# A mixture-of-experts router in three phases instead of two, with TensorE's table words loaded between the first blocks

## What is computed

```python
x = x + _L0_xattn_ref(_layernorm(x), ctx, ctx, mask, wo_w, wo_b)   # relu(softmax(q k + mask) v @ wo.T + b)
xf = _layernorm(x).reshape(-1, 256)
scores = softmax(xf @ gw + gb)                                     # (896, 32)
group_scores = sum(top_k(scores.reshape(T, 8, 4), 2))              # keep the 4 best groups
weights, indices = top 4 of the kept scores
for e in experts:  y += w_e * ((silu(xf @ w1e + b1e) * (xf @ w3e + b3e)) @ w2e + b2e)
z = (silu(xf @ sw1 + sb1) * (xf @ sw3 + sb3)) @ sw2 + sb2          # the shared expert
x = x + y + z
```

## Time and profile before

| | us |
|---|---|
| median of 3 runs | 327.31 (327.04 to 328.64) |
| the profiled execution, its own time | 327.03 |
| its span, first to last instruction | 325.3 |
| PE busy | 295.2 (91%) |
| DVE busy | 203.1 (62%) |
| ACT busy | 158.7 (49%) |
| POOL busy | 157.1 (48%) |
| stages of the span: attention to about | 146 |
| router of the last phase and shared expert to about | 192 |
| blocks to about | 303 |
| combination of the rows to | 325.3 |

### The profile page before, as it was taken

How to read it: one execution, slowest core, us unless ns; L and a number is a source line. 1 busy time by engine, 2 the same in 40 slices (tenths; PEclk the granted TensorE clock), 3 DMA queues, 4 the chain that set the end, 5 groups by cost and what they waited for, 6 DMA issues and landing times.

```text
span 325.3 us, 7289 instructions
## 1 busy us (share of the span) xinstructions
PE 295.2 (91%) x2311; PEld 206.5 (63%) x2311; DVE 203.1 (62%) x745; ACT 158.7 (49%) x429; POOL 157.1 (48%) x222
## 2 busy tenths in 40 slices
PE   7898999999999999989999927999999999999765
PEld 3566666666666766775555514777777787777443
DVE  2899775555596588977693121567876666666252
ACT  5575666666666476653411001445556765554001
POOL 8565435354544254416746740075555555555500
PEclk9999999999999999999599965899999999999999
DMA  7999496959793860008922332655554545552596
GB/s 195 228 151 303 140 308 187 306 141 298 221 334 96 259 201 2 2 3 305 371 75 72 121 120 42 87 154 156 161 155 154 163 147 163 161 164 81 174 286 187
DMA packets 56941, 55.92 MB, mean 172 GB/s; under 512 B 19165, under 2 KB 49386, under 8 KB 56394
## 3 DMA queue, kind: packets, MB, share of 16 engines
q1 hardware_dynamic: 52538, 43.94, 50.0%
q0 software_dynamic: 4368, 11.52, 10.6%
HBM read 35.03 MB, written 20.41 MB: 170 GB/s over the span
## 4 chain that ended last, share of the span: by engine, by line
PE 67%; DVE 12%; ACT 7%; DMA 5%; issue 4%; DVEq 3%; POOL 1%; SPq 0%; POOLq 0%
PE ps L1226 16%; PE ps L618 11%; PE ps L668 8%; PE ps L1241 7%; PE ps L681 6%; PE ps L1218 4%; ACT pT L803 4%; DVEq L1393 3%; DMA b<-expert_out 3%; PE ps L702 2%; PE ps L1235 2%; DVE z L906 2%; PE ps L591 2%; DMA expert_out<-hs,to 1%; PE ps L694 1%
## 5 line engine op out<-in xcount | busy, mean ns | idle before, releaser
L558 POOL TENSOR_SCALAR z<-z,zmax 112x375 f32<-112x375 f32 x96 | 55.7, 596 | 68.6 <-DVE zmax L906 68.6
L1158 POOL DMA_INDIRECT expert_out<-hs,to x59 | 56.6, 959 | 58.3 <-DVE hs L1404 35.7
L906 DVE CUSTOM_DVE_ANT_0 z<-ps,mask_sb 112x375 f32<-112x375 f32 x128 | 62.5, 544 | 33.7 <-PE ps L668 33.3
L803 ACT ACTIVATE pT<-ps 125x336 f32<-125x336 f32 x128 | 50.9, 449 | 39.0 <-PE ps L618 38.7
L1226 PE MATMUL ps<-w,xgT 128*128 x236 | 65.1, 400 | 3.3 <-ACT xgT L1305 3.3
L618 PEld LDWEIGHTS ps<-ident,z 112*125 112x125 f32 x384 | 47.3, 188 | 14.9 <-ACT pT L803 7.3
L618 PE MATMUL ps<-ident,z 112*125 112x112 f32 x384 | 56.6, 283 | 0.2 <-ACT pT L803 0.2
L1226 PEld LDWEIGHTS ps<-w,xgT 128*128 128x128 f32 x236 | 43.3, 197 | 15.2 <-issue 10.0
L1432 DVE TENSOR_TENSOR hb<-ps,b 128x256 f32<-128x256 f32 x59 | 25.1, 425 | 42.0 <-PE ps L1226 39.5
L402 POOL DMA_INDIRECT expert_rows<-normed,slots x32 | 30.6, 955 | 21.3 <-DVE normed L376 12.1
L1321 ACT COPY hs<-ps 128x128 f32<-128x128 f32 x59 | 15.7, 266 | 46.2 <-PE ps L1235 46.2
(11 more groups left out here) (207 smaller groups left out, 354.6 us busy)
## 6 DMA issues: line engine op xcount, KB each, us to landing
xg<-expert_rows SPq DMA_DIRECT2D x59, 128.0 KB, 2.3
expert_rows<-zero SPq DMA_DIRECT2D x14, 512.0 KB, 9.7
w2s<-in_L_ffn_w SPq DMA_DIRECT2D x2, 2048.0 KB, 9.3
b<-in_L_ffn_b SPq DMA_DIRECT2D x2, 2048.0 KB, 12.5
ctx_sb<-in_ctx SPq DMA_DIRECT2D x8, 336.0 KB
b<-expert_out SPq DMA_DIRECT2D x6, 448.0 KB, 6.6
mask_sb<-in_mask_Bx1xSxS_ff SPq DMA_DIRECT2D x8, 164.1 KB, 2.5
expert_out<-hs,to POOLq DMA_INDIRECT x59, 2.8
```

What stands on the lines that cost most here:

```text
L558: pool.tensor_scalar(z[:, n % RING, :], z[:, n % RING, :], -1.0, zmax[:, n % RING:n % RING + 1], ALU.mult, ALU.add).then_inc(by_pool, 1)
L803: nc.scalar.activation(pT[:, n % RING, :], ps[0:KP, T_BANK + at % 2, 0:KT * S], ACT.Exp).then_inc(ring_read, 1)
L906: nc.vector.tensor_tensor_reduce(out=z[:, n % RING, :], in0=ps[0:S, S_BANK + j, 0:SK], in1=mask_sb[:, b % 2, :], scale=-1.0, scalar=BIG, o ...
L1158: pool.indirect_dma_start(ys, bass.IndirectOffsetOnAxis(ap=to[:, j:j + 1], axis=0), y_sb[:, j % 4, :], None).then_inc(y_sent[j % 4], 16)
```

## The change

`PHASES` becomes three ranges of batches, 0 to 2, 3 and 4, 5 to 7. The first two have their transposes and logits inside the attention (iterations 18, 19 and 27, 28), and the first also its ranks (27 instead of 31). Every router step takes the width of its phase. Between two phases the state of the experts' rooms is carried on, so the middle phase needs a `more_blocks`, `more_keys`, `more_state` and `owners` of its own, and a `rank_and_count` of its own on PE in place of one filler matmul. POOL scatters 12, 8 and 12 times instead of 16 and 16. The constants that POOL writes for the router move from iteration 5 to iteration 3. `shared_up(1)` waits until DVE has read the middle phase's ranks. On PE one table word is loaded ahead of the first block, and 5, 5 and 4 behind the `up` of blocks 0, 1 and 2; the wait for `acc_ok` moves behind `up(1)`.

```diff
-    PHASES = ((0, B // 2), (B // 2, B))
-    PB = B // 2
-    ROUTED_AT = (("xT0", 22), ("xT1", 22), ("logit", 23), ("rank", 31))
-    EXP_AT = 25
-    FIRST_ROWS = 8
+    PHASES = ((0, 3), (3, 5), (5, 8))
+    LAST = PHASES[-1][0]
+    PB = max(hi - lo for lo, hi in PHASES)
+    ROUTED_AT = (("xT0", 0, 18), ("xT1", 0, 18), ("logit", 0, 19), ("rank", 0, 27),
+                 ("xT0", 1, 27), ("xT1", 1, 27), ("logit", 1, 28))
+    EXP_AT = (21, 30)
...
-                    elif p == QPB + 1:
+                    elif p == QPB - 1:
                         routing_constants()
-                pool.wait_ge(slots_ok, 2)
                 pool.wait_ge(xs_zero, 16 * (N_ZERO + 1))
-                for r, b in EARLY_ROWS[:FIRST_ROWS]:
-                    scatter_rows(pool, r, b)
+                scatter_phase(pool, 0)
+                scatter_phase(pool, 1)
...
                 turn_att(B - 1)
-                warm(1, S_BANK)
+                pe.wait_ge(sel_ok, 2)
+                rank_and_count(1, ps[:, S_BANK + 2, 0:wide(1) * E], ps[:, S_BANK + 3, 0:E]).then_inc(ranked, 1)
                 project(B - 1)
...
-                dve.wait_ge(ring_read, UNIT["rank", 0] + 1)
-                first_blocks(then_wait, ranks1[:, PB * E:(PB + 1) * E])
-                first_keys(then_wait, ranks1[0:S, 0:PB * E].rearrange("s (b e) -> s b e", e=E))
-                place(then_wait, 0)
-                variances(PB, B - 1)
-                first_state(then_wait, ranks1[:, PB * E:(PB + 1) * E])
+                choose_groups(then_wait, 1)
+                kept_scores(then_wait, 1)
+                sort_experts(then_wait, 1)
+                count_equals(then_wait, 1, E, restart)
+                choose_experts(then_wait, dve, 1)
+                variances(LAST, B - 1)
                 divide(B - 1)
...
-                owners(then_wait, 0)
+                owners(then_wait, 0, ends)
+                dve.wait_ge(ranked, 1)
+                more_blocks(then_wait, 1, ps[:, S_BANK + 3, 0:E], ends1, had, has)
                 residual(B - 1)
                 variances(B - 1, B)
                 inverses(B - 1, B, 3)
                 normalise(B - 1, x2, xn_ok)
+                more_keys(then_wait, 1, ps[0:S, S_BANK + 2, 0:wide(1) * E].rearrange("s (b e) -> s b e", e=E))
+                place(then_wait, 1)
+                more_state(then_wait, ps[:, S_BANK + 3, 0:E], has)
+                then_wait(owners(then_wait, 1, ends1))
+                banks_read()
...
-                for u in range(2):
-                    shared_up(u)
+                shared_up(0)
+                pe.wait_ge(ranks_read, 1)
+                shared_up(1)
...
-                words = [pe.value_load(word_i[0:1, n:n + 1], min_val=0, max_val=E ** 4 - 1) for n in range(NWORD)]
-                pe.wait_ge(acc_ok, B)
+                load_words(1)
...
                 for j in range(NBLK + 2):
                     if j < NBLK:
                         up(j)
+                    if j < TOPK - 1:
+                        load_words(1 + WORDS_EACH * (j + 1))
+                    if j == 1:
+                        pe.wait_ge(acc_ok, B)
```

More of the change, by code:

```diff
@@ L78, in closing @@
             units.append(("ctxT", b - 1))
[L79 removed]
+        return units + [(kind, f) for kind, f, at in ROUTED_AT if at == p]
     UNIT = {u: n for n, u in enumerate(ring_units())}
@@ L321, in chosen_weights @@
-        def chosen_weights(f):
-            lo, hi = PHASES[f]
-            TT(cw[:, lo:hi, 0:E], sc[:], sel[:, lo:hi, :].bitcast(F32), ALU.mult).then_inc(cw_ok, 1)
-        def every(ap):
-            return ap[0:S].unsqueeze(1).to_broadcast([S, PB, E])
-        def first_blocks(chained, counts):
+            lim = best[:, batches(f), count - 1:count].to_broadcast([S, wide(f), width])
+            TT(narrow(above, f, width), values, lim, ALU.is_gt)
+            chained(TT(narrow(equal, f, width), values, lim, ALU.is_equal))
@@ new lines, in count_equals @@
+        def count_equals(chained, f, width, starts):
+            n = wide(f)
+            nc.vector.tensor_reduce(n_above[:, 0:n], narrow(above, f, width), AX.X, ALU.add)
+            chained(nc.vector.tensor_tensor_scan(prefix[:].rearrange("s b e -> s (b e)")[:, 0:n * width],
+                                                 starts[:].rearrange("s b w -> s (b w)")[:, 0:n * width],
+                                                 narrow(equal, f, width).rearrange("s b w -> s (b w)"), 0.0, ALU.mult, ALU.add))
+            chained(TT(narrow(prefix, f, width), narrow(prefix, f, width), over_e(n_above[:, 0:n], [S, n, width]), ALU.add))
@@ L339, in first_keys @@
         def first_keys(chained, ranks):
[L340 to L342 removed]
+            k = key[:, batches(0), :]
+            chained(TT(k, ranks, every(base1[:], 0), ALU.add))
+            chained(TT(k, k, sel[:, batches(0), :].bitcast(F32), ALU.mult))
         def first_state(chained, counts):
[L346 removed]
@@ L347, in first_state, with more_blocks @@
             nc.vector.tensor_scalar(tail1[:], shift[:], float(PART), None, ALU.mult)
-            chained(nc.vector.scalar_tensor_tensor(room[:], had[:], float(PART), counts, ALU.mult, ALU.subtract))
-        def more_blocks(chained, counts):
+            chained(nc.vector.tensor_scalar(held[:], counts, 1.0, None, ALU.add))
+            chained(nc.vector.scalar_tensor_tensor(room[:], had[:], float(PART), held[:], ALU.mult, ALU.subtract))
+        def more_blocks(chained, f, counts, ends_, old, new):
@@ L352, in more_blocks @@
             chained(nc.vector.scalar_tensor_tensor(base1[:], held[:], -1.0, counts, ALU.add, ALU.add))
-            chained(TT(over[:], base1[:].unsqueeze(2).to_broadcast([P, E, LIM]),
-                       full[:].unsqueeze(1).to_broadcast([P, E, LIM]), ALU.is_gt))
-            chained(nc.vector.tensor_reduce(blocks[:], over[:], AX.X, ALU.add))
-            chained(TT(shift[:], blocks[:], had[:], ALU.subtract))
-            chained(nc.vector.tensor_tensor_scan(ends[:], ones_e[:], shift[:], 0.0, ALU.mult, ALU.add))
@@ L754, in _ @@
                 pe.wait_ge(xf_by_act, 2)
-                for b in range(PB, B - 1):
+                for b in range(LAST, B - 1):
                     route(pe, b)
@@ L1382, in _ @@
                 dve.wait_ge(counted, 1)
-                more_blocks(chained, ps[:, 6, 0:E])
-                more_keys(chained, ps[0:S, 5, 0:PB * E].rearrange("s (b e) -> s b e", e=E))
-                place(chained, 1)
-                owners(chained, 1)
+                more_blocks(chained, 2, ps[:, 6, 0:E], ends, has, blocks)
+                more_keys(chained, 2, ps[0:S, 5, 0:wide(2) * E].rearrange("s (b e) -> s b e", e=E))
+                place(chained, 2)
+                owners(chained, 2, ends).then_inc(owner_ok, 1)
                 shared_h(2)
```

357 lines of the change are left out of this document (200 added, 157 removed).

## The result

The changed kernel takes 338.0 us (median of 4 runs, 334.57 to 339.63) against 327.34 (327.04 to 328.64) for the kernel before on the same chip: ratio 1.027, 95% interval 1.022 to 1.032. It is slower, as forecast, but by 10.7 us instead of 1.9, outside the range of 325.5 to 331.8. The profiled execution was the quickest of the four (334.57 us, span 332.7); the later experiments come back to the other runs.

What follows compares the result with a forecast made beforehand. PE bounds the attention and blocks, DVE's chained steps and PE the stretch between; block 0's start and the first blocks' pace decide. At `up(5)` -1.7 - 0.2 + 2.8 + 1.0 = +1.9 us: 329.2 us, range 325.5 to 331.8.

Steps and rivals of the forecast that it cites:

- Constants: Iteration 5 of the attention: the normalising falls from 1.27 to 0.42 us without POOL's constants beside it, -0.7 us.
- Inside the attention: Iterations 25 to 31: DVE falls behind, PE loses 0.8 us at the ranks in 27; scores of 31 come +2.3.
- The rival with the slower DVE: Middle phase's steps in the attention hold the masks back two microseconds more: 331.2 us, slower; chance 0.13.
- DVE behind the attention: From the last mask, about 142.2 us, DVE's chain reaches the last phase's logits at 161.1, +4.6 us; its choice takes 8.0.
- The shared matmuls: Behind the last phase's ranks: 6.26 us as before, ending at 190.8 instead of 187.1.
- The gap ahead of block 0: 5.39 us of idle time goes, one word loading under queued matmuls; `turn_rows(0)` at 190.8 instead of 192.48, -1.7 us.
- Blocks 0 to 2: Word loads of 0.68 us each make the periods 4.7, 4.7 and 5.2, together 14.6 instead of 11.8: +2.8 us.
- The rival in which the words hide: PE takes the transposes while words load, blocks 0 to 2 stay at 11.8 us: -1.9, 325.4 us, faster; chance 0.10.
- The clock in the blocks: Lower clock through blocks 0 to 2, rising about 3 us after `up(3)`: `up(3)` to `up(5)` about 1.0 us longer.
- The scatters: POOL's last 12 scatters end at 189.2 us instead of 190.58, 1.4 gained, for which nobody waits.

Runs made afterwards that it cites:

- phases alone: The changed kernel with all fifteen word loads ahead of block 0 again, so only the three phases: 335.88 us, ratio 1.025 to the kernel before.
- the run with the ranks behind 28: The changed kernel with the first phase's ranks behind iteration 28 instead of 27 and `first_blocks` in 29, no filler: 332.37 us, ratio 1.013.
- the filler: The changed kernel with filler matmuls ahead of PE's waits for `sel` in iteration 27 and at the last phase's ranks: 332.23 us, ratio 1.011.
- the clock held up: The changed kernel with fillers ahead of both ranks' waits and three behind `up` of blocks 0, 1 and 2: 330.54 us, ratio 1.007.
- words alone: The kernel before with only its word loads changed to 1, 5, 5 and 4: 325.25 us, ratio 0.990.
- measured again: The changed kernel once more, with no edit, for another profile and more times: 336.54 us, ratio 1.026 to the kernel before.
- the quickest version: The kernel before with one word behind each `up`, constants in iteration 3, one filler behind the transposes of blocks 1 and 2: 318.04 us, ratio 0.969.
- one word each: One word load behind each `up`: on the kernel before 320.94 us, ratio 0.978; on the changed kernel 329.86 us, ratio 0.995.

## Why the prediction was right in direction and wrong in size

I compare with the profiled execution, of which the sum was made: 334.57 us measured, 328.9 predicted, 5.7 more. The median lies 3.4 us above it.

- **Constants**: -0.7 forecast, -0.6 measured. The normalising of iteration 5 came down to 0.66 us, not to 0.42; the next one took 0.7 longer, which PE did not feel. The Trainium skill, SBUF — State Buffer, in its reading of the diagram of ports, gives the shared port pair to one of VectorE and GpSimd for a whole instruction, but only for some kinds of VectorE instruction; a normalising of 1.27 us beside POOL's constants and of 0.66 without them agrees with a hold-up by POOL, and no run here tests the kind.
- **Inside the attention, the step that failed**: DVE's delay "costs PE 0.8 at the ranks in 27", so that "the scores of 31 come 3.0 later, less 0.7 for the constants: +2.3". They came 5.4 us later, 3.1 more. PE waited 1.39 us for `sel`, not 0.8, and in iteration 28 the clock behind that wait took 1.6 more (6.86 us against 5.25 in phases alone), which I had not considered there, although I had noted a dip near 155 us where PE made pauses of about 0.5. Of the rest, 0.4 is no part of the change: the first scores start at 6.68 us in the profile before and at 7.08 here and in most others. Iteration 28 took 0.3 more than the logits added to it even at full clock, and about 0.2 is spread over the others. I had also let DVE "fall behind by up to a microsecond" over seven iterations as if lead and delay carried over; the run with the ranks behind 28 shows that a lead does not. The rival with the slower DVE (331.2 us) had the place, the ranks in 27, but it gave all of its two microseconds to DVE, where without the clock and the later start about 1.1 were missing.
- **DVE behind the attention**: right. From the end of the masks to the last logits 18.9 us forecast, 19.25 measured; the choice 8.0 forecast, 7.94 measured. But the last mask ended at 145.4 us instead of the 142.2 forecast, so all of it is 3 us late or more. DVE sets it; PE takes its place when 5.9 us of steps are taken away, after 3.2.
- **The shared matmuls**: taken over at 6.26 us, measured 7.77. `sel` comes 1.88 us after PE has run out of work, where I had written that `shared_up(0)` and `(1)` end about a microsecond before it, and I gave the wait no price in clock. With the filler they took 6.26 us. A wait of 0.43 us ahead of the L1208 group is gone in return. So `turn_rows(0)` came at 195.36, not 190.8.
- **The gap ahead of block 0** closed, as forecast: the shared part follows on to the transposes.
- **Blocks 0 to 2**: 14.6 us forecast, 15.0 measured, 14.8 at full clock. The price of a load, 0.68 us with nothing beside it, is right. In sum `up(5)` came 4.9 us later than forecast: 3.2 from the attention up to the last mask, 0.3 from DVE behind it, 1.1 from the shared matmuls, 0.3 from the blocks. The rival in which the words hide is out: 3.4 us for five loads ahead of transposes whose rows were there. The Trainium skill, Advanced Engine Details and Errata, section Sequencer Loop, has engine instructions read and queued while a control instruction executes; these rows contradict that for register loads.
- **The clock in the blocks**: `up(3)` to `up(5)` 4.7 us forecast, 4.6 measured, 3.4 with the clock held up. I had it fall in the blocks and was right there; with the clock held up 1.2 us are gained here and nearly nothing in blocks 0 to 2.
- **The scatters**: 12 instead of 16; the last was issued 2 us later than before, at 192.5 instead of the 189.2 forecast, and nobody waited for it.
- Another 0.6 us is behind `up(5)`, where I had nothing.

What the runs left open: words alone gives -2.1 and phases alone +8.5, together 6.4, where the whole has 10.7 and, measured again, 8.8. The parts differ in where PE has idle time, and the dips behind it differ between executions of one kernel; how the 2.4 to 4.3 us that are left divide between the two was not settled. Nor was why a wait brings a dip in one execution and none in another: 1.39 us in the profile of phases alone and 2.85 in the quickest version brought none.

## What to carry to other kernels

Count a register load on the sequencer as blocking all that is written behind it on that engine, and place loads one at a time behind work that is long enough: in fives they gave 2.1 us, singly they gave 7. Splitting a chain of small dependent steps to start earlier can pay only if the engine that runs it has slack in every iteration it is put in; here 27 more steps stood ahead of the only result that was waited for, to shorten a transfer that nobody waited for. And price a new wait of TensorE of a microsecond or two at its own length, and as a risk at what follows at half the clock (1.5 us or more here, in most executions but not in all); a filler matmul queued ahead of it took that risk away in every profile here.

## What was not expected of the hardware

- Waits of 1.39 and 1.88 us between otherwise dense matmuls were followed by 3 us or more at 1.2 GHz, and cost 1.5 us or more each beyond the wait; but the same 1.39 us in one other execution, and 2.85 us in another kernel, were followed by none. Pauses of about 1.4 us in each 2.8 of the first blocks had the clock at 0.83 in the mean, with one short stretch at the lower level; with one filler of 1.0 us in each of two pauses it stayed at 2.4 GHz. The Trainium skill, TensorE: Matmul & The Clock Gate, section on a second HAM failure mode, tells of a kernel whose frequent small idle times made the clock go up and down; the profile of one word each on the kernel before agrees, while on the changed kernel the same pauses left it at 2.4 GHz.
- With three fillers behind each `up` the clock stayed at 1.00 through blocks 0 to 2; without them 9.75 us of PE's work in 13.7 did not raise it from 0.50. The window over blocks 1 to 4 of the run with words alone:

```profile
192.20:205.90 13.70, 9.75 (x27) 6.13 (x26) 1.43 (x4) 2.39 (x8) 0.00 (x0) 0.50 0.57 85
```

- With fillers the execution times of a kernel spread by 1.9 to 3.0 us; without them by 5.1 and 2.4 us for the changed kernel in its two measurements and by 7.3 with one word each. The kernel before spread by 3.0 to 4.9 us itself (one execution of 549 us aside), so the spread alone proves little.
